# A decoder layer on one core: seven experts scatter with accumulation into one area that starts as a copy of x2

## The reference

```python
N = B * S                                   # 4096
k = max(MIN_CAPACITY, ceil(N * 2.0 / E))    # 1024 tokens for each of 8 experts
scores = softmax(xt @ Wr, axis=-1)
G, idx = top_k(scores.T, k)
X_in = xt[idx]
h = gelu(einsum('ekd,edh->ekh', X_in, W1) + b1[:, None, :])
X_e = einsum('ekh,ehd->ekd', h, W2) + b2[:, None, :]
contrib = (G[..., None] * X_e).reshape(E * k, D)
out = zeros((N, D)).at[idx.reshape(-1)].add(contrib)
x3 = layernorm(x2 + out)
```

## Time and profile before

| what | value |
|---|---|
| median of the runs | 586.69 us |
| runs | 585.83, 586.69, 591.93 us |
| span of the profiled execution, first to last instruction | 585.1 us |
| busy share of the span | PE 94%, PE weight loads 73%, DVE 71%, ACT 56%, POOL 44% |
| bytes moved by DMA | 63.43 MB, of it HBM written 26.08 MB |

### The profile page before, as it was taken

One profiled execution on the slowest core, in us unless ns is written; L12 is line 12 of the kernel. 1 busy time (PEld: TensorE's weight loads), 2 busy tenths in 40 slices (PEclk: granted clock), 3 DMA queues, 4 the chain that ended last, 5 costly groups with the idle time before them and its releaser, 6 DMA issues.

```text
span 585.1 us, 11240 instructions
## 1 busy us (share of the span) xinstructions
PE 549.5 (94%) x3477; PEld 427.6 (73%) x3477; DVE 417.1 (71%) x1051; ACT 327.3 (56%) x670; POOL 260.2 (44%) x368
## 2 busy tenths in 40 slices
PE   8999999999999999999999898998999999999880
PEld 7868787888888788788878676566676575668530
DVE  3686786787687688668877875788758845656753
ACT  3577776767777677776767543442333525443133
POOL 4123524434352443435243430002777777777732
PEclk9999999999999999999999998998999999999985
DMA  7033442232234023423312404900223443665652
GB/s 242 2 82 91 135 117 52 96 109 97 47 115 134 25 83 115 112 50 115 104 60 65 150 10 144 304 2 11 55 57 106 138 129 121 191 194 163 221 185 108
DMA packets 62151, 63.43 MB, mean 108 GB/s; under 512 B 11809, under 2 KB 48930, under 8 KB 61858
## 3 DMA queue, kind: packets, MB, share of 16 engines
q1 hardware_dynamic: 58096, 55.37, 30.8%
q0 software_dynamic: 3584, 7.58, 4.6%
q10 hardware_dynamic: 434, 0.02, 0.0%
HBM read 36.85 MB, written 26.08 MB: 108 GB/s over the span
## 4 chain that ended last, share of the span: by engine, by line
PE 77%; DVE 13%; ACT 4%; issue 2%; POOL 1%; DMA 1%; POOLq 0%; DVEq 0%; ACTq 0%
PE PS L1577 17%; PE PS L1635 10%; PE PS L1607 9%; PE PS L1908 8%; PE PS L1930 7%; PE PS L1623 5%; PE PS L1821 4%; PE PS L1831 4%; DVE pc L1395 2%; DVE csum L1158 1%; ACT shared L891 1%; DVE cmax L1147 1%; PE PS L1681 1%; PE PS L1675 1%; PE PS L1667 1%
## 5 line engine op out<-in xcount | busy, mean ns | idle before, releaser
L767 POOL TENSOR_TENSOR pn<-pc,crcp 128x512 f32<-128x512 f32 (+1 forms) x93 | 80.4, 891 | 69.3 <-DVE crcp L1161 69.3
L1035 ACT ACTIVATE shared<-PS,b1T 128x512 f32<-128x512 f32 x88 | 60.5, 687 | 85.7 <-PE PS L1821 49.5
L807 POOL DMA_INDIRECT shared<-table,idx x56 | 54.3, 970 | 64.5 <-DVE idx L1402 48.0
L1607 PE MATMUL PS<-shared,x1T 128*128 128x512 f32 (+1 forms) x192 | 72.4, 513 | 1.2 <-ACT x1T L906 1.0
L817 POOL DMA_INDIRECT spread<-pn,idx x56 | 62.0, 1107 | 17.6 <-issue 15.6
L1607 PEld LDWEIGHTS PS<-shared,x1T 128*128 128x128 f32 x192 | 35.0, 189 | 37.6 <-issue 35.2
L862 ACT ACTIVATE shared<-PS 128x308 f32<-128x308 f32 x120 | 47.5, 428 | 25.5 <-PE PS L1577 25.2
L1147 DVE TENSOR_REDUCE cmax<-PS 128x16 f32<-128x1232 f32 x31 | 44.7, 1441 | 20.8 <-PE PS L1607 20.4
L1158 DVE TENSOR_REDUCE csum<-pc 128x16 f32<-128x1232 f32 x31 | 44.4, 1431 | 19.4 <-ACT pc L874 19.4
L1908 PE MATMUL PS<-pT,w 128*128 128x512 f32 x112 | 53.6, 611 | 3.3 <-ACT pT L1030 3.3
L1930 PEld LDWEIGHTS PS<-w,shared 128*128 128x128 f32 x448 | 51.7, 192 | 3.6 <-issue 3.1
(11 more groups left out here) (209 smaller groups left out, 1208.1 us busy)
## 6 DMA issues: line engine op xcount, KB each, us to landing
spread<-zeros SPq DMA_DIRECT2D x112, 128.0 KB, 2.0
shared<-spread SPq DMA_DIRECT2D x56, 256.0 KB, 4.3
xboth<-in_x SPq DMA_DIRECT2D x16, 256.0 KB, 2.7
w<-in_W SPq DMA_DIRECT2D x2, 1792.0 KB, 9.2
rest<-stage SPq DMA_DIRECT2D x56, 52.0 KB
table<-x SPq DMA_DIRECT2D x16, 128.0 KB, 1.9
fin<-table SPq DMA_DIRECT2D x1, 2048.0 KB, 18.2
out_x<-fin SPq DMA_DIRECT2D x8, 256.0 KB, 2.0
```

Of the source, the lines that this page charges most:

```text
L767: pool.tensor_tensor(pn[:, e, at_pn:at_pn + n * (b - a)].rearrange("p (h k) -> p h k", h=n), pc[:, e, :].rearrange("p (h k) -> p h k", h=H ...
L807: pool.indirect_dma_start(xg[:, e % 3, h, :], None, table, bass.IndirectOffsetOnAxis(ap=idx[:, e, h:h + 1], axis=0)).then_inc(gathered[e % ...
L1035: act.activation(hid[:, c, 512 * h:512 * h + 512], PS[:, HID_BANKS[k % len(HID_BANKS)], :], ACT.Gelu, bias=b1T[:, bias:bias + 1]).then_inc ...
L1607: i = pe.matmul(PS[:, n, 0:b - a], x1T[:, e, :], A[:, 2 * A_SLOT[phase] + e, a:b], start=True, stop=True)
```

## The change

One DRAM tensor `sums` takes the place of the seven areas. `store` writes each pair of x2 a second time, into `sums`. Every scatter adds to what stands there instead of writing (`compute_op=ALU.add`), and since two experts may pick the same token, the scatter of expert e waits until all eight DMAs of the scatter of e-1 have landed. `fin` holds the weighted dense expert alone; nothing is added to it on DVE. At the end SP loads `sums` once into `landed`, when the last scatter has landed, and PE adds `fin` and `landed` as before. Gone are the zeros and their clearing, the load of x2 from `table`, the loads of six areas and `add_landed`. SP no longer waits for POOL's constants at its start.

```diff
-            def clear(q):
-                for e in range(LISTED):
-                    sp.dma_start(to_clear[e][q], zeros[:, :]).then_inc(cleared, 16)
             def store(q, parity):
...
                 sp.dma_start(tab[q, :, :, 0:P], x2[parity][:, :, :]).then_inc(stored[parity], 16)
+                start_of_sums = sums.rearrange("(t q e) d -> q t e d", e=2, t=P)
+                sp.dma_start(start_of_sums[q, :, :, :], x2[parity][:, :, :]).then_inc(stored[parity], 16)
...
-            sp.wait_ge(consts, 18)
             attention_steps(sp, step)
...
-            sp.dma_start(fin[:, :, :], by_token[:, :, 0:P]).then_inc(fin_x, 16)
-            for e in range(LISTED):
-                sp.wait_ge(scattered[e % 2], 16 * SB * (e // 2 + 1))
-                rows = spread[e].rearrange("(t b) d -> t b d", t=P)
-                for c in range(B // 4):
-                    if e:
-                        sp.wait_ge(landed_added, B // 4 * (e - 1) + c + 1)
-                    sp.dma_start(landed[:, 4 * c:4 * c + 4, :], rows[:, 4 * c:4 * c + 4, :]).then_inc(landed_in[c], 16)
+            sp.wait_ge(scattered[(LISTED - 1) % 2], 16 * SB * ((LISTED - 1) // 2 + 1))
+            by_token = sums.rearrange("(t b) d -> t b d", t=P)
+            for c in range(B // 4):
+                sp.dma_start(landed[:, 4 * c:4 * c + 4, :], by_token[:, 4 * c:4 * c + 4, :]).then_inc(landed_in[c], 16)
...
             def scatter(e):
-                if e == 0:
-                    pool.wait_ge(cleared, 16 * LISTED * PAIRS)
+                if e:
+                    pool.wait_ge(scattered[(e - 1) % 2], 16 * SB * ((e - 1) // 2 + 1))
                 for h in range(SB):
                     pool.wait_ge(ye_done, blocks_through(e, h))
-                    pool.indirect_dma_start(spread[e], bass.IndirectOffsetOnAxis(ap=idx[:, e, h:h + 1], axis=0),
-                                            ye[:, e % 2, h, :], None).then_inc(scattered[e % 2], 16)
+                    rows = bass.IndirectOffsetOnAxis(ap=idx[:, e, h:h + 1], axis=0)
+                    pool.indirect_dma_start(sums, rows, ye[:, e % 2, h, :], None,
+                                            compute_op=ALU.add).then_inc(scattered[e % 2], 16)
...
-                    wait(dve, stored[par], 16 * earlier)
+                    wait(dve, stored[par], 32 * earlier)
...
-                for b in range(4 * g, 4 * g + 4):
-                    i = dve.scalar_tensor_tensor(out=fin[:, b, :], in0=xall[:, b, :], scalar=weight[:, b:b + 1],
-                                                 in1=fin[:, b, :], op0=ALU.mult, op1=ALU.add)
-                i.then_inc(dense_added, 1)
+                dve.tensor_tensor(fin[:, 4 * g:4 * g + 4, :], four,
+                                  weight[:, 4 * g:4 * g + 4].unsqueeze(2).to_broadcast([P, 4, P]),
+                                  ALU.mult).then_inc(dense_added, 1)
...
             for c in range(B // 4):
-                pe.wait_ge(landed_added, B // 4 * (LISTED - 2) + c + 1)
+                pe.wait_ge(dense_added, c + 1)
                 pe.matmul(PS[:, c, :], ident[:, :], fin[:, 4 * c:4 * c + 4, :].rearrange("p b d -> p (b d)"),
                           start=True, stop=False)
             for c in range(B // 4):
-                pe.wait_ge(landed_in[c], 16 * LISTED)
+                pe.wait_ge(landed_in[c], 16)
```

More of the change, by code:

```diff
@@ L342, in decoder_layer @@
         idx = sb("idx", [P, E, SB], I32)
-        zeros = sb("zeros", [P, 2 * P])
         stf = sb("stf", [P, B, 6])
@@ L456, in decoder_layer @@
         table = nc.dram_tensor("table", [TOKENS, ROW], F32, kind="Internal").ap()
-        spread = [nc.dram_tensor(f"spread{e}", [TOKENS, P], F32, kind="Internal").ap() for e in range(LISTED)]
+        sums = nc.dram_tensor("sums", [TOKENS, P], F32, kind="Internal").ap()
         rest = nc.dram_tensor("rest", [PAIRS // PHASES, 2 * PHASES, HEADS, KEYS_REST, P], F32, kind="Internal").ap()
         rest_pairs = rest.rearrange("r (q e) (c h) k d -> (r q) (h k) e c d", e=2, c=2)
-        to_clear = [t.rearrange("(q p e) d -> q p (e d)", q=PAIRS, p=P) for t in spread]
         def ring_wait_free(eng, at, name):
@@ L641, in step @@
                     load_rest(at, p + 1, 1 - parity, 4 * PHASES * groups)
-                if runs("cross", first):
-                    clear(p)
                 if runs("post", first):
@@ L722, in _ @@
             pool.memset(keep[:, :, :], 1.0).then_inc(consts, 1)
-            pool.memset(zeros[:, :], 0.0).then_inc(consts, 1)
             pool.memset(onesb[:, :], 1.0).then_inc(consts, 1)
-            pool.wait_ge(consts, 17)
+            pool.wait_ge(consts, 16)
             pool.memset(keep[:, :, 0:1], 0.0).then_inc(consts, 1)
@@ L1430, in results, with dense_add @@
                                   ALU.mult).then_inc(ye_done, 1)
-            added = [0]
-            def dense_add(g, landed_before):
+            def dense_add(g):
                 if g == 0:
-                    dve.wait_ge(fin_x, 16)
                     dve.wait_ge(b2b_in, 16)
                 dve.wait_ge(dense_out, g + 1)
-                if landed_before:
-                    dve.wait_ge(landed_added, landed_before)
                 four = xall[:, 4 * g:4 * g + 4, :]
                 link(dve.tensor_tensor(four, four, b2b[:, DENSE:DENSE + 1, :].to_broadcast([P, 4, P]), ALU.add))
-                for b in range(4 * g, 4 * g + 4):
-                    i = dve.scalar_tensor_tensor(out=fin[:, b, :], in0=xall[:, b, :], scalar=weight[:, b:b + 1],
-                                                 in1=fin[:, b, :], op0=ALU.mult, op1=ALU.add)
-                i.then_inc(dense_added, 1)
-                added[0] += 1
-            def add_landed(e, first, last):
-                if e == 0 and first == 0:
-                    dve.wait_ge(fin_x, 16)
-                if added[0]:
-                    dve.wait_ge(dense_added, added[0])
-                for c in range(first, last):
-                    dve.wait_ge(landed_in[c], 16 * (e + 1))
-                    if e:
-                        dve.wait_ge(landed_added, B // 4 * (e - 1) + c + 1)
-                    dve.tensor_tensor(fin[:, 4 * c:4 * c + 4, :], fin[:, 4 * c:4 * c + 4, :],
-                                      landed[:, 4 * c:4 * c + 4, :], ALU.add).then_inc(landed_added, 1)
+                dve.tensor_tensor(fin[:, 4 * g:4 * g + 4, :], four,
+                                  weight[:, 4 * g:4 * g + 4].unsqueeze(2).to_broadcast([P, 4, P]),
+                                  ALU.mult).then_inc(dense_added, 1)
             take(0, 1)
@@ L1479, in _ @@
                     make_idx(e + 3)
-                if e >= 2:
-                    add_landed(e - 2, 0, B // 8)
                 results(e, 1)
-                if e >= 2:
-                    add_landed(e - 2, B // 8, B // 4)
                 if e < 2:
                     for k in range(IN_ROUTING // 2 * e, IN_ROUTING // 2 * (e + 1)):
-                        dense_add(k, 0)
+                        dense_add(k)
                 if e - 1 in TAIL:
-                    dense_add(TAIL[e - 1], B // 4 * (e - 1))
-            add_landed(LISTED - 3, 0, B // 4)
+                    dense_add(TAIL[e - 1])
             last_results()
-            add_landed(LISTED - 2, 0, B // 4)
             def fin_shift(c):
```

10 lines of the change are left out of this document (3 added, 7 removed).

## The result

| | before | after |
|---|---|---|
| median | 588.41 us (4 runs, 585.83 to 591.93) | 615.22 us (4 runs, 613.42 to 617.53) |
| span of the profiled execution | 585.1 us | 613.3 us |

The ratio is 1.046, with a 95% interval from 1.0404 to 1.0517: the change makes the kernel slower by 4.6%. The forecast was 587.0 us in a range from 583.0 to 600, so the result lies outside it. Ratios and intervals here are taken over runs in the faster of the chip's two states, while a median in the first set of experiments also holds some slower ones.

A forecast was written before the change was run, and what follows sets the result against it. PE was taken to bound attention and the experts, POOL's full queue and the last scatter's landing the end. Terms +0.1, +0.4 and -0.3 made +0.2 on 585.1 us, plus 1.6 to the median: said 587.0 us, range 583.0 to 600.

The forecast's parts named there:

- Step 3: POOL's issue of each adding scatter: taken as 1.02 us, 0.05 more than plain, with bounds of 0.97 and 1.94 us.
- The first rival: POOL's unbroken queue: x us more per adding scatter costs 54 x less 2.8 us against the sum; chance 0.30.
- Step 1: Clearing DMAs on SP's queue in attention go, second x2 stores come: taken as 0, with a gain of at most 3.5 us.
- Less than 7 us of idle PE in attention: Sign in the attention stretch that would show the rival of a real gain from less DMA traffic; 7.0 us idle before.
- Step 2: DVE loses 30.4 us of additions, hidden by PE; POOL regains some 2.1 us; last expert's results could begin at about 539.6 us.
- Step 4: Wait for the scatter ahead, uncovered only between experts 5 and 6: landing 3.5 us, 0.9 us won, 1.0 given back, +0.1.
- long landing: Landing of adding scatters: at 6.5 us both uncovered landings pay, +6 us, 593 us; chance 0.08.
- serial wait: Additions run one after the other behind gathers in POOL's queue, five more boundaries of some microseconds; given little chance.
- Step 5: End of kernel: same loads, 3.13 us to the first, PE idle about 3.0 us, +0.4 for a slightly longer cold stretch.
- relief rival: Landing 2.3 us, no added POOL price, half of PE's attention idle won back: some -6.5 us, 580.5 us; chance 0.08.
- the forecast's own range: Whole kernel, the forecast case without its rivals: 583.5 to 591 us; chance 0.47.

The follow-up runs named there:

- first set of experiments: On a slower chip: changed kernel with plain scatters, 634.78 us; kernel before with adding scatters, 629.66 us, and with the waits too, 633.05 us.
- price list: Changed kernel with experts 0 to 5 each given another form of scatter (128 or 64 rows, full or half rows, plain or adding), expert 6 plain; one run, 628.86 us.
- chip of section 2: Chip like the first, kernel before 586.53 us; there changed kernel with plain scatters took 583.79 us, kernel before with adding scatters 615.02 us.
- chip of section 4: Chip where the kernel before took 586.84 us (29 runs); kernel before with plain scatters and only the new waits took 588.18 us, ratio 1.0021.

## Why the prediction was wrong

**Step 3, the price of an adding scatter, failed.** I took 1.02 us; it is 1.55. The row for it was missing from the trace; I had bounds of 0.97 and 1.94, and chose the lower end, as "the nearest row is the plain scatter". That argument has a hole. Gathers and scatters both only move rows, and that they cost the same says nothing of an addition. Where bounds lie twofold apart and the price is multiplied by 54, the choice is the forecast, and the nearest row is no measurement of what the rows don't contain.

**The rest of the sum held, and so did the rival's formula.** The first rival gave 54 x less 2.8 us against my sum. With x = 1.55 - 0.97 = 0.58 it gives 28.5 us, and my sum was a span of 585.3. The measured span is 613.3 us, 28.0 above that. (2.2 of these come from the late start, so that the change itself is 25.8 and the formula high by 2.7.) It had a chance of 0.30, and I let its size end at x = 0.3 in the range, though my own upper bound went to 0.97. A range that takes in the bounds would have reached beyond 615 us: by the same formula 0.97 gives 49.6 us.

**A rule against the choice was at hand.** POOL held 1.55 us for each adding scatter here, against 0.97 for a plain one. The Trainium skill, page "Collectives: The Full Stack", section "The bandwidth ceiling: the fold count and why AG ≠ RS ≠ AR", has two read descriptors for a reducing step, from which the prediction made an estimate of 1.46 us by way of three descriptors for two. That is 0.09 us from the measured price; but the prices of 64 and 128 rows, 1.41 and 1.57 us, show that most of it doesn't grow with rows, so the nearness isn't a proof of that mechanism. What POOL does in the added 0.58 us no run here shows.

**Step 1, clearing costs nothing:** right. PE is busy in attention for 328.47 us against 327.96. ("Less than 7 us of idle PE in attention" was to show the relief; it is 6.5, and no gain came of it, so that sign was set too close.)

**Step 2, DVE's relief:** right in kind. PE hid DVE. The lengthened scatters beside additions did go: 56 plain ones take 62.0 us before and 56.0 in the changed kernel with plain scatters. Up to expert 5 POOL gained 3.3 us of idle time, where I had counted 2.1. With the additions gone and plain scatters, the last expert's results start at 539.21 us (539.6 forecast), but its scatters only at 543.96, when those of expert 5 have landed. So of the 5.4 us by which the results came earlier, 1.6 us were left.

**Step 4, the new wait:** right. I took 3.5 us for the landing (median 3.3, and 3.33 and 3.19 us at the two places that nothing covers), and covers of 10, 7.5 and 2.5 us for experts 1 to 5, where indeed no wait shows. Ahead of expert 6 I expected some 3 us of idle time (my own times make it 545.3 less 542.8, 2.5 us; measured 2.04 with the gap). The long landing and the serial wait as rivals fall. My sentence that the other waits stay covered up to 7 us of landing was wrong for expert 5, where I had a cover of 2.5 us; at 3.3 us it didn't matter.

**Step 5, the end:** the loads took the same 3.14 us. PE's idle time ahead of them grew to 13.37 us instead of 3.0, with POOL's delay, yet its last sixteen matmuls took 8.72 us against 8.83, so the +0.4 us for a longer stretch at the lower clock isn't seen.

**The relief rival** is right in part once the price of adding is taken away: 583.79 us against 586.53, a gain of 2.7. I had given 6.5, of it 3.5 for half of PE's idle time in attention, which nothing gave back. The lower end of the forecast's own range, 583.5, is also a slip: 586.9 less 2.4 less 0.7 is 583.8.

## What to carry to other kernels

Before you let a DMA do arithmetic, price the instruction on the engine that issues it: the copying engines have room (this queue's share of them rose to 9.6% only), the issuer may not. Here 0.58 us on 56 instructions outweighed 27 MB of traffic (63.43 to 36.14 MB) and 34 us of DVE time (417.1 to 383.6 us busy), because POOL, busy for 44% of the whole span, had no slack in one stage; look at the idle time before each instruction of the stage, not at the share. And when a price is multiplied by fifty, give the range both of its bounds.

## What the runs showed of the hardware beside this

**The packets of an adding scatter go with its rows, and the price on POOL doesn't.** POOL's DMA queue before is in the earlier trace rows; after it is (packets, MB, share of 16 engines):

```profile
q0 software_dynamic: 9856, 7.58, 9.6%
```

The bytes are the same 7.58 MB. Before, an indirect DMA had 32 packets (3584 / 112). The 6272 more are 112 for each of 56 scatters, so an adding one has 144: room for one packet for each of its 128 rows of 512 bytes, and 16 others. The kernels with 24 and with 8 adding scatters have 6272 and 4480 packets, again 112 more for each. The price list has 5760; if a plain scatter of 64 rows has 32 packets too, an adding one of 64 rows has 80, again its rows and 16 (an estimate). POOL's price falls only from 1.57 to 1.41 us with it. The queue's share of the DMA engines makes 0.24 us for a plain indirect DMA (4.6% of 585.1 us over 112) and, with the gathers at that, some 0.81 us for an adding scatter. That is 3.4 times as much, where the prediction allowed for twice; at 1.85 us from issue to issue it still bounds nothing.

**DVE's additions with both inputs in SBUF lengthen POOL's plain scatters more than its adding ones.** A plain one takes 0.97 us alone and up to 1.53 us in the kernel before; 56 of them together are 7.7 us too long. In order of time every one over 1.05 us overlaps a DVE instruction, mostly an addition, though some that overlap one are not lengthened (522.36 us: 0.97). The adding ones of the kernel before, beside the same additions (89.4 us for 56, against 86.8 at 1.55 us each), lose 2.6 us. The Trainium skill, page "SBUF — State Buffer", section "Who interferes with whom", says that a tensor_tensor with both inputs in SBUF contends with what GpSimd reads, and infers that descriptor generation is not touched by it. The first of these is in keeping with the rows; the inference is not: with the additions gone, and POOL's list otherwise alike but for the waits, 6.0 of the 7.7 us went. The loads of the areas went with them, but they aren't the cause of all of it: at 442.78 us a scatter takes 1.47 us beside `dense_add`, before the first of these loads (448.3 us).

**The start of the program varies by up to 5 us, and TensorE's clock goes with it.** On the chip of section 2 the runs of one kernel fall into groups some 4 to 5 us apart (with plain scatters eight at 583.4 to 584.2 and two at 588.0 to 588.2 us; with three adding experts two at 593.5 to 593.7 and two at 597.7 to 597.9 us), the later ones at the lower mean clock. On the chip of section 4 the runs of the kernel before fill the space between (585.27 to 590.81 us). PE's clock from 10 to 14 us after the start, before:

```profile
10.00:12.00 2.00, 2.00 (x24) 1.88 (x24) 0.69 (x4) 0.53 (x2) 1.04 (x5) 1.00 0.68 203
12.00:14.00 2.00, 1.62 (x18) 1.43 (x16) 1.44 (x3) 1.56 (x3) 0.00 (x0) 1.00 0.59 210
```

in the changed kernel:

```profile
10.00:12.00 2.00, 1.91 (x9) 1.69 (x9) 0.00 (x0) 0.42 (x2) 1.07 (x4) 0.56 0.69 250
12.00:14.00 2.00, 2.00 (x16) 2.00 (x17) 0.69 (x4) 0.04 (x1) 0.37 (x2) 0.59 0.40 110
```

and in the kernel before with adding scatters and waits:

```profile
10.00:12.00 2.00, 1.67 (x9) 1.44 (x9) 0.00 (x0) 0.67 (x2) 1.08 (x4) 0.69 0.92 353
12.00:14.00 2.00, 2.00 (x13) 2.00 (x13) 0.69 (x4) 0.00 (x0) 0.36 (x2) 0.50 0.43 123
...
20.00:22.00 2.00, 2.00 (x13) 2.00 (x13) 0.54 (x2) 0.86 (x2) 0.00 (x0) 0.75 0.00 0
```

The granted clock is at its upper level (1.00, 2.4 GHz) throughout in the first. In the other two it falls to the lower one (0.50, 1.2 GHz) between 10 and 12 us; it is back at 1.00 from 14 us in the second and only from 22 us in the third. Up to 10 us it is 1.00 in all three, and from 4 to 10 us PE was busy for 5.03, 5.12 and 5.37 us in this order, so the two that fall hadn't been the idler ones. The first scatter then comes at 436.31, 438.49 and 441.11 us. Plain and adding versions show both, with and without the waits, so it isn't the change; what decides it wasn't tried. It adds to the difference of the two profiled spans, 2.2 of 28.2 us, and a comparison of two single profiles should first be aligned on a row behind the start.

**On one chip every kernel was slower behind attention.** The kernel before took 624.97 us there and 586.5 to 588.4 on the others. In attention PE is busy for 328.45 of 335 us there too (the changed kernel with plain scatters; 328.02 on the chip of section 2); from 412 to 546 us it is 108.55 us against 130.01. PE stands idle on "issue" between matmuls that wait for nothing the trace names. There the price of adding made the kernel before 5 us slower instead of 28. Why that chip differs, and whether late instructions are behind these gaps, stays open.
